# A two-layer graph kernel with a streamed adjacency matrix: two late ring slots, a listed order for its last stage, and a shorter way through its last block row

## The reference

```python
def layer0(x, adj, u):
    keep = (u >= 0.1).astype(x.dtype)
    return adj @ (x * keep / 0.9)

def layer1(x, adj, kernel, bias):
    n = clip(norm(x), 0, 10);       x_proj = tanh(n) * x / (n + 1e-8)
    s = adj @ x_proj
    n = clip(norm(s), 0, 0.999);    out = arctanh(n) * s / (n + 1e-8)
    return out @ kernel + bias

x = layernorm(x + layer0(x, adj, u))
x = layernorm(x + layer1(x, adj, kernel, bias))
```

## Time and profile before

| | us |
|---|---|
| median of 3 runs (946.13 to 947.37) | 946.2 |
| the profiled execution, its own time | 946.4 |
| its span (first to last instruction recorded) | 944.2 |
| PE busy within the span | 898.7 (95%) |
| DVE busy | 283.0 (30%) |
| ACT busy | 53.2 (6%) |
| POOL busy | 56.9 (6%) |
| DMA moved | 358.35 MB, mean 380 GB/s |

### The profile page before, as it was taken

One profiled execution on the slowest core, in us unless ns is written; L12 is line 12 of the kernel. 1 busy time (PEld: TensorE's weight loads), 2 busy tenths in 40 slices (PEclk: granted clock), 3 DMA queues, 4 the chain that ended last, 5 costly groups with the idle time before them and its releaser, 6 DMA issues.

```text
span 944.2 us, 10549 instructions
## 1 busy us (share of the span) xinstructions
PE 898.7 (95%) x4224; PEld 322.4 (34%) x4224; DVE 283.0 (30%) x1046; ACT 53.2 (6%) x138; POOL 56.9 (6%) x49
## 2 busy tenths in 40 slices
PE   5669999999999999999999999999999999999993
PEld 1113333333333333333333444444444444443331
DVE  1134574322314130304040221203121030336644
ACT  0000110000000000000000000000000000013322
POOL 0000000000000000000000000000000000003322
PEclk9999999999999999999999999999999999999997
DMA  9999999999999999997979998997989979899992
GB/s 369 414 421 420 421 421 420 421 422 421 421 421 421 421 417 422 380 423 258 424 237 413 390 363 320 341 423 283 407 290 370 422 269 362 336 423 421 421 422 108
DMA packets 53328, 358.35 MB, mean 380 GB/s; under 512 B 6305, under 2 KB 8353, under 8 KB 10401
## 3 DMA queue, kind: packets, MB, share of 16 engines
q1 hardware_dynamic: 50544, 355.49, 93.4%
q10 hardware_dynamic: 2736, 2.20, 0.7%
HBM read 355.57 MB, written 2.10 MB: 379 GB/s over the span
## 4 chain that ended last, share of the span: by engine, by line
PE 83%; DMA 7%; DVE 3%; SPq 2%; ACT 2%; POOL 1%; issue 1%; ACTq 0%; POOLq 0%; DVEq 0%
PE sums_both L629 38%; PE sums_first L583 20%; PE sums_part L592 16%; DMA ring<-adj_dram 7%; PE sums_part L583 4%; PE sums_both L611 3%; PE sums_part L611 3%; SPq L313 1%; ACT xres L363 1%; POOL rooted L330 1%; DVE stats L425 1%; SPq L309 1%; DVE y L541 1%; SPq L308 0%; DVE mv L428 0%
## 5 line engine op out<-in xcount | busy, mean ns | idle before, releaser
L629 PE MATMUL sums_both<-ring,feats 128*64 128x512 f32 x1696 | 370.3, 592 | 0.5 <-DMA ring<-adj_dram 0.5
L583 PE MATMUL sums_first<-ring,feats 128*64 128x512 f32 x1088 | 246.6, 599 | 28.4 <-DMA ring<-adj_dram 28.4
L629 PEld LDWEIGHTS sums_both<-ring,feats 128*64 128x64 f32 x1696 | 136.7, 137 | 228.0 <-issue 226.0
L592 PE MATMUL sums_part<-ring,feats 128*64 128x512 f32 x880 | 193.3, 593 | 0.0
L583 PEld LDWEIGHTS sums_first<-ring,feats 128*64 128x64 f32 x1088 | 78.8, 138 | 189.3 <-issue 140.1
L435 DVE TENSOR_TENSOR row_saved<-sums_both,row_saved 64x512 f32<-64x512 f32 x15 | 10.2, 683 | 349.3 <-ACT row_saved L383 349.2
L592 PEld LDWEIGHTS sums_part<-ring,feats 128*64 128x64 f32 x880 | 66.9, 137 | 119.0 <-issue 118.2
L340 POOL TENSOR_TENSOR rooted<-base,power 128x8 f32<-128x8 f32 x16 | 27.8, 1735 | 795.7 <-DVE base L462 795.7
L492 DVE TENSOR_TENSOR support<-sums_part,support 128x512 f32<-128x512 f32 x36 | 24.9, 692 | 139.2 <-PE sums_part L592 139.1
L583 PE MATMUL sums_part<-ring,feats 128*64 128x512 f32 x208 | 48.5, 595 | 2.8 <-DMA ring<-adj_dram 2.8
L383 ACT COPY row_saved<-sums_first 64x512 f32<-64x512 f32 x16 | 9.3, 580 | 600.4 <-PE sums_first L583 600.4
(11 more groups left out here) (64 smaller groups left out, 236.1 us busy)
## 6 DMA issues: line engine op xcount, KB each, us to landing
ring<-adj_dram SPq DMA_DIRECT2D x335, 1024.0 KB, 12.9
xres<-x_dram SPq DMA_DIRECT2D x8, 256.0 KB, 17.0
support<-u_dram SPq DMA_DIRECT2D x8, 256.0 KB, 16.8
out_dram<-xres ACTq DMA_DIRECT2D x16, 128.0 KB, 7.5
selw<-selector_dram ACTq DMA_DIRECT2D x1, 32.0 KB, 3.4
selw<-weight_dram ACTq DMA_DIRECT2D x1, 32.0 KB, 3.7
bias_sb<-bias_dram ACTq DMA_DIRECT2D x1, 32.0 KB, 6.1
```

The lines of the kernel that those rows point to most:

```text
L583: last = nc.tensor.matmul(bank[at:at + F], feats[:, c * TB + t, which, :], ring[:, slot, t, :], start=start and t < 2, stop=stop and t >= ...
L592: last = nc.tensor.matmul(bank[F * g:F * g + F], feats[:, c * TB + t, 1, :], ring[:, slot, t, :], start=start and t == 0, stop=stop and t ...
L629: last = nc.tensor.matmul(sums_both[r % 2][layer * F:layer * F + F], feats[:, c * TB + t, layer, :], ring[:, slot, t, :], start=begin and ...
```

## The change

1. `feats` is laid out layer by layer (`[P, 2, NT, F]` for `[P, NT, 2, F]`). Its layer-0 half is not read after row 15 of layer 0, and two blocks fit into it: `SPARES = 2` slots, which `place_blocks` adds to the free list at the first `part` after `turn` 15. PE adds two to `block_released` there.
2. The residual is written in place into `xres`. `y` shrinks to 4 tiles, and the wait of `residual` for the stores' `out_ready` goes.
3. `HELD`, `REREAD` and `EARLY_RUN` have other values. The last stage's groups are a list (`FINISHED`), and so are the units between one `finish` and the next (`GAPS`).
4. Row 5, the last: once row 4 is projected, POOL clears row 4's half of `support`. Then one 128-partition addition puts both halves of the bank in, and the projection contracts 128 rows, which adds the halves (`selector` and `weight` were on both halves already).
5. The last row's normalisation is split: ACT does tiles 0 and 1 and stores them, DVE tiles 2 and 3, which SP stores. Row 4's normalisation on ACT moves behind the square of row 5.
6. The host puts x and u side by side, and one DMA brings a chunk of both.

```diff
-EARLY_RUN = 3
-FINISH_EVERY = 3
-FINISH_LAG = 1
-HELD = [4, 4, 4, 3, 5, 4, 3, 4, 6, 5, 4, 3, 3, 2, 2, 1]
-REREAD = [0, 0, 0, 0, 0, 0, 1, 3, 3, 0, 8, 0, 4, 0, 2, 0]
+SPARES = 2
+EARLY_RUN = 5
+HELD = [4, 4, 4, 3, 5, 4, 3, 5, 6, 5, 4, 3, 3, 2, 1, 1]
+REREAD = [0, 0, 0, 0, 0, 0, 0, 4, 3, 1, 5, 0, 5, 0, 2, 0]
+FINISHED = [(12, 13), (10, 11), (14, 15), (8, 9), (6, 7), (2, 3), (0, 1), (4,), (5,)]
+GAPS = [6, 2, 3.5, 4.5, 4, 8, 5, 5, 5]
...
         if kind != "hold":
             freed += [slot for slot, _ in held]
+        if turned == NB and kind == "part" and not spares:
+            spares = SPARES
+            freed += range(SLOTS, SLOTS + SPARES)
...
-                    sp.dma_start(xres[:, t, :], x[:, t, :]).then_inc(chunk_loaded[chunk], 16)
-                    sp.dma_start(keep[:, t, :], u[:, t, :]).then_inc(chunk_loaded[chunk], 16)
+                    sp.dma_start(rows_in[:, :, t, :], xu[:, chunk]).then_inc(chunk_loaded[chunk], 16)
...
+            tiles = slice(final * TB + TB // 2, final * TB + TB)
+            sp.wait_ge(final_halved, 1)
+            sp.dma_start(out[:, tiles, :], xres[:, tiles, :]).then_inc(out_stored, 16)
...
+                    if k == mate_done:
+                        pool.wait_ge(rows_projected, k + 1)
+                        nc.gpsimd.memset(support[half(final ^ 1), final // 2], 0.0).then_inc(mate_cleared, 1)
                     pool.wait_ge(squares_summed, k + 1)
...
+                if k == len(groups) - 1:
+                    tiles = slice(final * TB, final * TB + TB // 2)
+                    for i in range(TB // 2):
+                        last = nc.scalar.activation(xres[:, final * TB + i, :], xres[:, final * TB + i, :], ACT.Identity,
+                                                    scale=rooted[:, 0, i:i + 1], bias=shift[:, i:i + 1])
+                    last.then_inc(out_ready, 1)
+                    act.wait_ge(out_ready, rows_before(k) + 1)
+                    act.dma_start(out[:, tiles, :], xres[:, tiles, :]).then_inc(out_stored, 16)
+                    return
...
+                    if k == len(groups) - 1:
+                        normalise(k - 1)
                     act.wait_ge(log_asked, k + 1)
...
-                if len(rows) == 2:
+                if n == final_part:
+                    dve.wait_ge(mate_cleared, 1)
+                if len(rows) == 2 or n == final_part:
...
-                if k >= 2:
-                    dve.wait_ge(out_ready, rows_before(k - 1))
...
+            k = len(groups) - 1
+            dve.wait_ge(deviation_ready, 2 * k + 1)
+            for i in range(TB // 2, TB):
+                last = V.tensor_scalar(xres[:, final * TB + i, :], xres[:, final * TB + i, :], mv[:, i, 0:1],
+                                       rooted[:, 0, i:i + 1], ALU.subtract, ALU.mult)
+            last.then_inc(final_halved, 1)
...
-                    last.then_inc(block_released, len(r))
+                    last.then_inc(block_released, len(r) + (SPARES if i == first_reread else 0))
...
+                    for t in range(TB if rows == (final,) else 0):
+                        last = nc.tensor.matmul(projected[finished % 2][0][:, t, :],
+                                                support[:, final // 2, t * P:(t + 1) * P],
+                                                selw[:], start=True, stop=True)
```

More of the change, by code:

```diff
@@ L126, in work_order @@
     order += reread(LEAD, last) + column(last)
-    pairs = sorted(range(NB // 2), key=lambda p: 2 * NB - reread_to[2 * p] - reread_to[2 * p + 1])
     groups = []
-    for pair in pairs[:-1]:
+    for together in FINISHED:
         steps = []
         while True:
-            rows, low, high = behind(pair, NB)
-            if not rows:
+            low = min(reread_to[r] for r in together)
+            rows = tuple(r for r in together if reread_to[r] == low)
+            if low == NB:
                 break
+            high = min([NB] + [reread_to[r] for r in together if r not in rows])
             steps += partial(rows, range(low, high), False)
@@ L137, in work_order @@
                 reread_to[r] = high
-        groups.append(((2 * pair, 2 * pair + 1), steps))
-    for row in (2 * pairs[-1], 2 * pairs[-1] + 1):
-        groups.append(((row,), partial((row,), range(reread_to[row], NB), False)))
-    ended, since, now = [], 0, 0
-    for rows, steps in groups:
+        groups.append((together, steps))
+    ended = since = 0
+    for g, (_, steps) in enumerate(groups):
         for step in steps:
             order.append(step)
-            now += len(step[1])
             since += len(step[1])
-            if ended and since >= FINISH_EVERY and now - ended[0][1] >= FINISH_LAG:
-                order.append(("finish", ended.pop(0)[0]))
-                since = 0
-        ended.append((rows, now))
-    for rows, _ in ended:
+            if ended < g and since >= GAPS[ended]:
+                order.append(("finish", groups[ended][0]))
+                ended, since = ended + 1, 0
+    for rows, _ in groups[ended:]:
         order.append(("finish", rows))
@@ L200, in build @@
     groups = [s[1] for s in order if s[0] == "finish"]
+    first_reread = order.index(("turn", NB - 1)) + 1
     last_part = {r: s[3] for s in order if s[0] == "part" for r in s[1]}
+    final = groups[-1][0]
+    mate_done = next(k for k, rows in enumerate(groups) if final ^ 1 in rows)
+    final_part = last_part[final]
     def rows_before(k):
@@ L258, in build @@
         early_banks = [sums_both[0], sums_part[PARTS - 1]]
-        block_loaded = [sem(f"block_loaded{i}") for i in range(SLOTS)]
+        block_loaded = [sem(f"block_loaded{i}") for i in range(SLOTS + SPARES)]
         chunk_loaded = [sem(f"chunk_loaded{i}") for i in range(NT // CHUNK)]
@@ L290, in build, with block_of @@
         block = es.enter_context(nc.Block())
+        def block_of(slot):
+            return ring[:, slot] if slot < SLOTS else spare[:, slot - SLOTS]
         def half(r):
@@ L459, in layer1_end @@
                 done(V.tensor_tensor(y[:, own, :], turned[:], xres[:, rows, :], ALU.add))
-                moments(y, TB)
+                moments([y[:, t, :] for t in range(TB)])
                 done(V.tensor_scalar(base[:, 0, own], mv[:, own, 1], LN_EPS, None, ALU.add))
@@ L547, in residual @@
                     dve.wait_ge(deviation_ready, 2 * k)
-                moments(yk, tiles)
+                moments([xres[:, r * TB + t, :] for r in groups[k] for t in range(TB)])
                 V.tensor_scalar(base[:, 0, own], mv[:, own, 1], LN_EPS, None, ALU.add)
@@ L582, in two_halves @@
                     at = F * (t % 2)
-                    last = nc.tensor.matmul(bank[at:at + F], feats[:, c * TB + t, which, :],
-                                            ring[:, slot, t, :],
+                    last = nc.tensor.matmul(bank[at:at + F], feats[:, which, c * TB + t, :],
+                                            block_of(slot)[:, t, :],
                                             start=start and t < 2, stop=stop and t >= TB - 2)
@@ L591, in two_rows @@
                     for g, slot in enumerate(slots):
-                        last = nc.tensor.matmul(bank[F * g:F * g + F], feats[:, c * TB + t, 1, :],
-                                                ring[:, slot, t, :],
+                        last = nc.tensor.matmul(bank[F * g:F * g + F], feats[:, 1, c * TB + t, :],
+                                                block_of(slot)[:, t, :],
                                                 start=start and t == 0, stop=stop and t == TB - 1)
```

57 lines of the change are left out of this document (31 added, 26 removed).

## The result

| | before | after |
|---|---|---|
| median, on one chip together (6 runs each) | 947.5 us | 942.6 us |
| ratio to before, 95% interval | | 0.9952 [0.9939, 0.9965] |
| profiled execution, its own time | 946.4 us | 942.4 us |
| its span | 944.2 us | 939.8 us |

The change is 4.9 us faster by the medians and 4.0 us by the two profiled executions. The forecast was 941.6 us and 4.6 us less. In a later batch of five runs the median of the changed kernel was 943.8 us, 3.6 us under the 947.4 us of the kernel before beside it. So a median moves by about 1 us from batch to batch, and smaller differences are read from the traces here. A trace has limits too: it shows one execution of several, and not always the middle one.

A forecast was written before the change was run, and what follows sets the result against it. PE's matmuls were taken to bound the middle, waits for loads the end. Terms 2.8 + 0.7 + 0.7 + 0.4 = 4.6 us off 946.4 gave 941.8, stated as a 941.6 us median; range 939.3 to 944.4.

The forecast's parts named there:

- the tables: Last stage: new step order puts one load ahead (2.5 us) and one row's store fewer before the last load (0.3 us).
- One addition: Row 5's end on DVE: one 128-partition addition for two saves 0.7 us; POOL's clear takes some 0.54 us.
- split normalisation: Last row's end: ACT normalises two tiles instead of four, 0.7 us less; nothing given for the smaller or second store.
- x and u together: Kernel start: one DMA issue fewer puts the first block earlier and the end gains the same, 0.4 us.
- the spare slots: Last stage: two slots given to loads 299 and 300 when DMA already runs at full rate, worth nothing; upper end 5.0 us.
- The bound: Whole kernel: PE's matmuls set the middle at 1.717 us a unit; waits for loads cost 3.9 us near the end.
- rival B: Kernel end: no wait for loads is left, DVE's row 4 work limits row 5's addition to 925.8; 940.1 us, chance 0.17.
- The waits for DVE: PE's earlier last-stage projections: two waits, 0.64 and 0.16 us, likely go with wider gaps, but the load still sets the end.
- the list of signs: Trace marks expected after the change, among them row 5's projection 1.2 us after its last block and a clear of about 0.5 us.
- Rival C: Row 4's chain: POOL's clear exceeds 1 us idle plus 0.8 us spare and slows the kernel, up to some 1020 us; chance 0.04.
- Rival D: Middle, rows 7 to 11: fewer slots turn over and PE starves, a gap of 2.5 us, about 944 us; chance 0.07.
- A gap on PE between 210 and 860 us: Middle of the kernel: a sign that, if seen in the trace after, would make the prediction wrong; no size given.

The follow-up runs named there:

- all the rest: Changed kernel with the earlier HELD, REREAD, EARLY_RUN and last-stage order put back, everything else kept: 944.7 us, ratio 0.9974 to the kernel before.
- The stretch without stores: Changed kernel without the stores of its first six groups, so 12 of 16 block rows are never written: 940.8 us.
- the one with an earlier slot: Changed kernel with the first spare slot freed after `both` (15, 7), 26 us before `turn` 15, the second as before: 940.3 us, ratio 0.9929.
- the order alone: Kernel before with only the change's HELD, REREAD, EARLY_RUN and listed last stage: 945.6 us for 947.7 us, ratio 0.9977.
- the two without slots: Changed kernel with SPARES = 0, run twice: 943.2 us, then 943.77 us beside 943.79 us for the change.
- the run with two: Changed kernel with two 64-partition additions and a 64-row projection for row 5, without POOL's clear: 943.4 us.
- The eight clears: Changed kernel with row 4's half of `support` cleared eight times in sequence on POOL instead of once: 942.9 us.

## Why the prediction was right

The total was right (4.9 us for 4.6), its parts less so, and part of the agreement is luck. By the runs above, the order gave 2.2 us where the tables had 2.8, and all the rest gave 2.7 us where it had 1.8. One addition and the split normalisation make 1.4 us of the 2.7 in the traces, x and u together nothing. The other 1.3 us are open: the spare slots, the residual in place, for which there is no run by itself, and the 1 us by which medians move.

*The bound.* It held: PE's 1.717 us a unit in the middle, loads at the end. The stretch without stores shows the next bound, DVE at 925.2, where the forecast's rival B had 925.8. B's time of 940.1 us is also about where the one kernel without waits for loads (940.8 us) and the one with an earlier slot (940.3 us) came out. The range's lower end, 939.3 us, should have been 939.5 us by its own terms (940.1 less the other 0.6 us of the start).

*The tables, 2.8 us.* The last block started 2.90 us earlier, but not by the tables alone. They gave 1.1 us in the trace of the order alone and 1.3 and 0.6 us in the two without slots. The step that failed is "at 820 DMA turns to its own rate with one load fewer to go". The count was right up to 819.3 (280 slots freed for 279). It was not carried on: before, a pair's step frees numbers 280 and 281 together at 822.7, and after, a single row's step frees number 281 at about the same time (822.6), so that the lead is gone there but for the spare slots. And DMA wasn't at its own rate then; after the change it moved 303 GB/s up to 825, as `turn` 15 stands three units later. A single lead in slots was thus worth less than one load. The 0.3 us for one row's store fewer isn't to be seen: 12 rows' stores are issued by 916.0 before and by 915.0 after, and the 13th shortly ahead of the last block in both, at 925.8 and 924.3.

*The spare slots, nothing.* Wrong, by the same moment: "by then DMA runs at its full rate, held back by no slot". They come at about 822, and DMA was paced up to 825. The reason given was wrong; the cost may still have been about right. Their worth is 1.7 us between the traces with and without them and 0.0 to 0.6 us between the medians, and chance can make most of the 1.7. The forecast's upper end, that slots given sooner are worth up to a load each, agrees with the early slot, 2.3 to 3.4 us for one slot and 2.5 us for one load. Its time is also where DVE becomes the bound, so that it can't show more. The sum of the two terms, 2.8 us, matches the 2.90 us of the first trace at the last block. The six traces with both slots and the new order lie 2.0 to 3.2 us under the kernel before, so that match is in part chance.

*The waits for DVE, 0.8 us.* Those of the earlier projections went, as the wider gaps made likely. This didn't shorten the end, because the load still set it.

*One addition, 0.7 us.* Right: 0.72 us between before and after, 0.73 us by the run with two. The projection comes 0.79 us after the last block's end, as this term gives it (1.5 - 0.7); the 1.2 us in the list of signs doesn't fit the term. The clear read 0.52 us for the 0.54 us taken from the two small clears of the earlier trace rows.

*Split normalisation, 0.7 us.* Right in the trace, 0.66 us to the last issue. DVE's two tiles ran from 936.68 to 937.22 and POOL's shift from 936.73 to 936.93, and the shift took 0.20 us as it does alone. The Trainium skill's "SBUF — State Buffer", section Who interferes with whom, has the two lock each other out where the `tensor_scalar` runs in a 2-port mode. No such wait is seen here, and the trace doesn't say in which mode DVE's two ran.

*x and u together, 0.4 us.* Wrong: nothing. The step that failed is "what the start gains, the end gains". The first block moved, and 65 us later PE stood where it had stood. From 10 us to 73 us DMA moves 411 to 423 GB/s in every stretch of 10 us, before and after, so there the bytes set the time, not the first issue.

*Rival C* had its point of decision wrong. It gave the clear some 1.8 us of cover. The eight clears took 4.54 us and cost nothing, so the cover is at least that. *Rival D* came up in a small way: a gap of 0.2 to 0.6 us near 505 us in four of the eleven traces with the change's order, and in neither of the two with the old one. A gap on PE between 210 and 860 us was among the signs that would make the prediction wrong. The first trace of the change had none, its second had 0.24 us, far below the 2.5 us that D was priced at. What causes it is open.

## What to carry to other kernels

A buffer slot is worth something only at moments at which transfers wait for slots, so give it as early as its old content is dead, and look at the transfer rate at that very moment in the changed order, not in the old one. Where a lead in slots is counted, follow the count on until the transfers run at full rate. And before an operation is charged to a chain, look at what the waiting engine does at the time: 4.5 us on POOL were covered, most of it by DVE's own work.

## What the runs showed that was not expected

The profiled execution can be off its kernel's other executions by more than the effect under study. With the early slot it took 942.1 us and the other four 940.2 to 941.2; without slots it took 944.7 us in the repeat, for a median of 943.8; with the order of before they agree (944.7 and a median of 944.7). So before two traces are compared, put the time of each one's own execution beside the median of its kernel.

DMA's lead varies between executions of one program. The two traces of the change differ by 0.5 us at the last block, and PE has gaps at 207.38 (0.31 us) and 504.83 (0.24 us) in the one and none in the other.

DVE's `tensor_scalar` on 128 x 64 floats from SBUF to SBUF with two per-partition operands took 0.31 us a tile, 0.54 us for two, and ACT's two tiles 0.77 us.
